# Second layer's deformable sampling: nine products summed by transposes that accumulate in PSUM, tap weights by blocks of 128, x tents in PSUM

## The reference, cut to what matters

```python
xi = xg[:, :, :, g, :]
offsets = conv_same(xi, w_off[g], b_off[g])
# sample_with_offsets: loc = grid + kernel_grid + offsets, clipped to the image
interp = w_(wa) * Ia + w_(wb) * Ib + w_(wc) * Ic + w_(wd) * Id     # bilinear, 9 points x 16 channels
h = depthwise_same(sampled, w_dw[g], b_dw[g])                      # H x W x 144
outs.append(conv_same(h, w_pw[g], b_pw[g]))                        # 144 -> 16
```

## Time and profile before

| what | us |
|---|---|
| median of 3 runs (lowest, highest) | 295.47 (294.94, 296.95) |
| span of the profiled execution | 295.1 |
| PE busy over the span | 234.4 (79%) |
| DVE busy | 196.2 (66%) |
| POOL busy | 140.1 (47%) |
| ACT busy | 57.0 (19%) |

### The profile page before, as it was taken

One profiled execution on the slowest core, in us unless ns is written; L12 is line 12 of the kernel. 1 busy time (PEld: TensorE's weight loads), 2 busy tenths in 40 slices (PEclk: granted clock), 3 DMA queues, 4 the chain that ended last, 5 costly groups with the idle time before them and its releaser, 6 DMA issues.

```text
span 295.1 us, 2939 instructions
## 1 busy us (share of the span) xinstructions
PE 234.4 (79%) x908; PEld 134.6 (46%) x910; DVE 196.2 (66%) x476; ACT 57.0 (19%) x94; POOL 140.1 (47%) x196
## 2 busy tenths in 40 slices
PE   0959298988988789978883586889899788899990
PEld 0725096763336642224531142457578746343430
DVE  7767779979875387573309859998977144326286
ACT  1411924210001164513111000010101301310100
POOL 5300009786951509713404929999996010000560
PEclk9997969999996579999995769999999997799997
DMA  3529970000000000000166000000000000000000
GB/s 114 160 50 187 203 196 0 0 0 3 1 1 0 0 1 3 0 0 0 26 154 125 0 1 0 0 1 3 0 0 0 2 0 0 1 2 0 0 18 18
DMA packets 5759, 9.37 MB, mean 32 GB/s; under 512 B 2390, under 2 KB 2926, under 8 KB 5742
## 3 DMA queue, kind: packets, MB, share of 16 engines
q1 hardware_dynamic: 5742, 9.18, 13.3%
HBM read 7.48 MB, written 1.69 MB: 31 GB/s over the span
## 4 chain that ended last, share of the span: by engine, by line
PE 40%; DVE 30%; POOL 15%; issue 6%; ACT 5%; DMA 1%; DVEq 1%; POOLq 0%; ACTq 0%
POOL ring L265 12%; PE ps L1011 5%; PE ps L906 5%; PE ps L746 4%; PE ps L764 3%; DVE ps L1176 3%; PE ps L876 3%; DVE big L279 3%; PE ps L932 2%; DVE cm L1123 2%; DVE xn L1079 2%; PE ps L699 2%; PE ps L813 2%; DVE ring L287 2%; PE ps L727 2%
## 5 line engine op out<-in xcount | busy, mean ns | idle before, releaser
L265 POOL TENSOR_TENSOR ring<-big 128x384 f32<-128x384 f32 x72 | 59.2, 861 | 9.4 <-PE ps L906 4.6
L297 POOL TENSOR_TENSOR big<-big 128x512 f32<-128x512 f32 x30 | 32.0, 1095 | 38.6 <-ACT big L621 32.9
L906 PE MATMUL ps<-ring,ident 128*128 128x384 f32 x100 | 38.0, 523 | 10.2 <-POOL ring L265 5.7
L746 PE MATMUL ps<-ring,ident 128*128 128x192 f32 x126 | 26.4, 362 | 8.6 <-DVE ring L287 8.4
L1484 DVE TENSOR_TENSOR ps<-ps,ring 128x384 f32<-128x384 f32 x46 | 25.8, 562 | 9.6 <-PE ps L906 8.4
L906 PEld LDWEIGHTS ps<-ring,ident 128*128 128x128 f32 x100 | 19.1, 202 | 26.3 <-DVE ring L265 7.2
L746 PEld LDWEIGHTS ps<-ring,ident 128*128 128x128 f32 x126 | 22.6, 208 | 12.8 <-DVE ring L287 12.8
L433 POOL TENSOR_TENSOR rstd<-veps,mhalf 128x4 f32<-128x4 f32 x8 | 8.3, 1032 | 39.3 <-DVE veps L1075 39.2
L691 PE MATMUL ps<-zero,ident 128*128 128x512 f32 x34 | 22.7, 815 | 1.6 <-DVE big L1402 1.6
L554 POOL TENSOR_TENSOR big<-big 128x256 f32<-128x256 f32 (+1 forms) x12 | 7.6, 635 | 34.4 <-DVE big L1562 33.7
L265 DVE TENSOR_TENSOR ring<-big,ps 128x384 f32<-128x384 f32 x36 | 19.5, 546 | 0.1
(11 more groups left out here) (270 smaller groups left out, 397.5 us busy)
## 6 DMA issues: line engine op xcount, KB each, us to landing
big<-pad SPq DMA_DIRECT2D x8, 392.0 KB, 9.5
big<-pad SPq DMA_DIRECT2D x8, 240.0 KB, 5.5
w<-in_w_dram SPq DMA_DIRECT2D x2, 512.0 KB
w<-in_w_dram SPq DMA_DIRECT2D x2, 256.0 KB
pad<-img SPq DMA_DIRECT2D x8, 64.0 KB, 2.1
pad<-zero SPq DMA_DIRECT2D x1, 484.0 KB, 3.9
pad<-zero SPq DMA_DIRECT2D x1, 400.0 KB, 4.5
x<-in_x_dram SPq DMA_DIRECT2D x1, 256.0 KB, 2.6
```

The costliest lines, as they stand in the source:

```text
L265: return eng.tensor_tensor(V(ring, 0, slot * SP, [[1, P], [NJ * C, 3], [C1, NJ * G1], [1, C1]]), bigv((py + dy) * SLAB1 + (dx + j0) * C, [ ...
L297: return eng.tensor_tensor(dst, bigv(wy * SLAB0 + wx * C, [C0, J * G0], [1, C0]), table, ALU.mult)
L746: return mm(bank(px + dx, 0, P, [1, 3 * J * G0], off=dy * J * G0), ident[:, :], ring[:, slot + 3 * px * J * G0:slot + 3 * (px + 1) * J * G ...
L906: mm(bank(1 + i % 2, 0, P, [1, SP]), ident[:, :], ring[:, slot * SP:slot * SP + SP], start=(n == 0), stop=(n == len(srcs) - 1)).then_inc(s ...
```

## The change

The items are gone. A chunk of two columns is handled whole: nine terms, one for each shift d, each with all nine points of both columns. A term is two products of 576 numbers per partition (`sample_product`, one for each column), written so that the group's 9 x 16 samples lie in one run of 144. Five shifts are on DVE (0 to 4), four on POOL (5 to 8): 40 and 32 products. Nothing is added on DVE. PE instead transposes every term and lets the transposes accumulate in PSUM: per term nine 128 x 128 blocks (`add_term`, L896 of the changed file), in the order of `TERMS`; banks 1, 2 and 3 hold the chunk's nine transposed blocks, ACT copies them after the ninth term, and the next chunk's first term waits for these copies.

The blocks of 128 rows cut across the runs of 144, so that each group and column lies in two adjoining blocks. `taps_out` (L925 of the changed file) has two products for each, 16 per chunk, with weights `w_u` laid out by blocks, zero outside. Twelve of a chunk's 16 are put between the terms of the next chunk by `TAPS_BY`, four come after it.

The tents: the x tents are written to PSUM (bank 4), so that `pair_weights` reads one operand from SBUF and one from PSUM. The lower tent is left negative and the sign is put in by a `scalar_tensor_tensor` with -1. A partition with an offset over 1 gets weight 0 (`near`), which adds two one-number operations and one of 576. The reduction of the largest offset stands ahead of the pairs instead of behind them; POOL's product with -1 goes away. The two weight loads (52 KB, and twice 6.5 KB) become one of 209 KB (128 x 408 numbers), at the same place in SP's order; POOL's preparation becomes one product of 2304 numbers and two of 64.

```diff
+            def transposed_sum(dst, columns, first, last):
+                return mm(dst, columns, ident[:, :], is_transpose=True, start=first, stop=last, skip_group_check=True)
+            def add_term(ci, t):
+                who = TERMS[t]
+                k = ci * TERMS.count(who) + TERMS[:t].count(who)
+                first, last = t == 0, t == len(TERMS) - 1
                 for n in range(NJ):
+                    if first and ci:
+                        pe.wait_ge(sem("st"), (NJ + 1) * (ci - 1) + n + 1)
+                    pe.wait_ge(sem("s_pool" if who == "pool" else "s_dve"), NJ * k + n + 1)
                     for g in range(G1):
+                        done = transposed_sum(bank(1 + n, 0, P, [1, P], off=g * P),
+                                              term_slot(who, k, (n * G1 + g) * P, [1, P]), first and g == 0, last)
+                    if last:
+                        done.then_inc(sem("st_ps"), 1)
+                if first and ci:
+                    pe.wait_ge(sem("st"), (NJ + 1) * ci)
+                done = transposed_sum(bank(3, 0, P, [1, P]), term_slot(who, k, NJ * G1 * P, [1, P]), first, last)
+                done.then_inc(sem("s_pe"), 1)
...
             pe.wait_ge(sem("tents1"), 1)
             keep_clock(3, 3)
+            for ci in range(NC):
+                if ci > 1:
+                    for part in range(TAPS_BY[-1], TAP_PARTS):
+                        taps_out(ci - 2, part)
+                for t in range(len(TERMS)):
+                    add_term(ci, t)
+                    if ci:
+                        for part in range(TAPS_BY[t], TAPS_BY[t + 1]):
+                            taps_out(ci - 1, part)
+            for part in range(TAPS_BY[-1], TAP_PARTS):
+                taps_out(NC - 2, part)
+            for part in range(TAP_PARTS):
+                last = taps_out(NC - 1, part)
+            last.then_inc(sem("u_ps"), 1)
...
-            v.scalar_tensor_tensor(bigv(T1 + 2 * NT, [1, NT]), u1[:, :], 0.0, val1[:, :], ALU.max, ALU.mult)
-            dve.wait_ge(sem("neg_val1"), 1)
-            v.scalar_tensor_tensor(bigv(T1, [1, NT]), u1[:, :], 0.0, ml[:, :], ALU.min, ALU.mult)
+            for dst, half in ((x_tent1, of_x), (y_tent, of_y)):
+                v.scalar_tensor_tensor(dst(2), u1[:, half], 0.0, fx[:, half], ALU.max, ALU.mult)
+                v.scalar_tensor_tensor(dst(0), u1[:, half], 0.0, fx[:, half], ALU.min, ALU.mult)
...
-SP = 3 * NJ * C
+SP = NJ * K * C
-S_DVE = (0, 1, 2)
-S_POOL = (3, 4, 5, 6, 7, 8)
+POOL_SLOTS, DVE_SLOTS = 4, 5
+S_DVE = (0, 1, 2, 3, 4)
+S_POOL = (5, 6, 7, 8)
+TERMS = ("pool", "dve", "pool", "dve", "dve", "pool", "dve", "dve", "pool")
+TAP_PARTS = 2 * NJ * G1
+TAPS_BY = (0, 0, 2, 4, 5, 6, 8, 9, 10, 12)
```

More of the change, by code:

```diff
@@ L125, in program @@
         flagf = sb("flagf", P, 4)
+        near = sb("near", P, 2)
         flagi = sb("flagi", 1, 4, dt=I32)
@@ L202, in program @@
         aby = sb("aby", P, J * GP0)
-        BIG = 19760
+        BIG = 18432
         big = sb("big", P, BIG)
@@ L275, in pair_weights, with y_tent, x_tent1 @@
+        def y_tent(k):
+            return bigv(T1 + k * J * GP1, [1, J * GP1])
+        def x_tent1(k):
+            return bank(4, 0, P, [1, J * GP1], off=k * J * GP1)
         def pair_weights(eng, d):
             dy, dx = divmod(d, 3)
[L278 to L281, removed]
+            dst = bigv(AD + d * J * GP1, [1, J * GP1])
+            if (dy == 0) != (dx == 0):
+                pair = eng.scalar_tensor_tensor(dst, y_tent(dy), -1.0, x_tent1(dx), ALU.mult, ALU.mult)
+            else:
+                pair = eng.tensor_tensor(dst, y_tent(dy), x_tent1(dx), ALU.mult)
+            pair.then_inc(sem("pairs"), 1)
@@ L335, in _ @@
             load(b_of[:, :], "b_of", "w_of")
-            load(w_ta[:, :], "w_ta", "w_dp")
-            for hf in range(2):
-                load(w_tb[C * hf:C * hf + C, :], "w_tb", "w_dp")
+            load(w_t[:, :], "w_t", "w_dp")
             load(b_tb[C:C + 1, :], "b_pw", "w_dp")
@@ new lines, in add_term, with taps_out @@
+                done.then_inc(sem("s_pe"), 1)
+            def taps_out(ci, part):
+                ng, tail = part % (NJ * G1), part // (NJ * G1)
+                n, g = divmod(ng, G1)
+                j = NJ * ci + n
+                block = ng + tail
+                if part in (0, G1, TAP_PARTS - 1):
+                    pe.wait_ge(sem("st"), (NJ + 1) * ci + (1, 2, 3)[block // G1])
+                return mm(bank(4 + g, 0, P, [1, K * C1], off=j * 3 * C1), bigv(ST + (ci * 9 + block) * P, [1, P]),
+                          w_u[:, (ng * 2 + tail) * K * C1:(ng * 2 + tail + 1) * K * C1], start=(j == 0 and tail == 0),
+                          stop=(j == J - 1 and tail == 1), skip_group_check=True)
@@ L1511, in _ @@
+                sampling(general=True)
+            with dve.Else():
+                sampling(general=False)
             dve.wait_ge(sem("u_ps"), 1)
@@ L1776 @@
     b_dw = i["L1_conv_b_dw"].reshape(G1, K, C1).transpose(1, 2, 0)
-    w_ta = np.concatenate([t[:8].reshape(P, -1) for t in (w_dw, w_pw, b_dw)], axis=1)
-    w_tb = np.concatenate([np.moveaxis(t[8], 1, 0).reshape(C, -1) for t in (w_dw, w_pw, b_dw)], axis=1)
+    w_t = np.zeros((3, P, 2 * NJ * G1, C1), np.float32)
+    for ng in range(NJ * G1):
+        for e in range(K * C1):
+            block, row = divmod(ng * K * C1 + e, P)
+            part, (p, c) = 2 * ng + block - ng, divmod(e, C1)
+            w_t[0, row, part, :K] = w_dw[p, c, ng % G1]
+            w_t[1, row, part] = w_pw[p, c, ng % G1]
+            w_t[2, row, part, 0] = b_dw[p, c, ng % G1]
+    w_t = np.concatenate([w_t[0, :, :, :K].reshape(P, -1), w_t[1].reshape(P, -1), w_t[2, :, :2 * G1, 0]], axis=1)
     data = {
```

323 lines of the change are left out of this document (91 added, 232 removed).

## The result

The changed kernel takes **280.52 us** (median of 5 executions, 278.67 to 281.08) against 294.94 us before (5 executions, 293.1 to 296.95) on the same chip: ratio 0.951, 95% interval 0.9456 to 0.9564. The prediction was 279.5 us, with 275 to 290 as its range.

The account below looks back on a forecast made before the run. The prediction took POOL's 72 products to bound the old stage and PE the new one. Moving the last tap from 234.3 to 218.3 us saves 16.0: 295.1 - 16.0 = 279.1 us span, 279.5 against the median, range 275 to 290.

Parts of the forecast that it names:

- The bound and its size: Sampling: PE becomes the bound at 12.8 us per chunk; last tap at 218.3 against 234.3 us, 16.0 us less.
- The far end: Upper bound for one POOL product of 576 numbers in the sampling: 1.6 us, for addressing in four dimensions.
- POOL idle waiting for PE, over 3 us per chunk: Sign expected in the sampling's trace: POOL stands idle behind PE for over 3 us in each chunk.
- Pairs: DVE's nine pair products before the sampling: 0.39 us each, 3.5 us instead of 7.9.
- if that cure fails they cost 7.9 again: Fallback for DVE's nine pairs: without the gain from a PSUM operand they take 7.9 us, 4.4 more.
- The branch: Flag and branch between pairs and copy of weights: 0.65 us, bounds 0 and 1.3, against 1.45 before.
- keep_clock: PE's start of the sampling, when keep_clock is done: 5.3 us after the tents, at 166.3 us.
- What was to cost nothing: Larger weight load, under 1 us if uncovered; POOL's preparation of 4.6 us, ready early; work after the last tap unchanged.
- Clock falls under transposes: Rival, sampling: PE's clock drops to 0.50 and stays there, last tap at 263, total 328 us; chance 0.13.
- It falls in the first chunk: Rival: PE's clock drops only in the first chunk, without taps between transposes; 7.3 us more, 287 us; chance 0.07.
- Weight loads as the pace: Rival, PE's transposes: each goes at its weight load's 0.14 us; 9.7 us more, 289 us; chance 0.05.
- POOL the bound: Rival, sampling: POOL's products take above 1.6 us and still bound it; at 1.8 us the total is 285; chance 0.02.

Follow-up runs that it names:

- e8: Changed kernel with only the split of the nine products moved, VectorE four and POOL five instead of five and four: 279.57 us, ratio 0.9499.
- e3: Changed kernel with the three x tents in SBUF instead of PSUM, all else the same: 281.49 us, ratio 0.9526.
- e1: Changed kernel without the three 512-column products on zeros (keep_clock) ahead of the sampling: 281.07 us, ratio 0.9501.
- e2: Changed kernel with all 64 taps behind the last transpose, so 324 transposes in a row: 280.12 us, ratio 0.9496.
- e6: Changed kernel with VectorE adding two of its five products of a chunk in SBUF, so PE sums eight terms: 279.65 us, ratio 0.9505.
- e7: Changed kernel with VectorE taking six products, POOL three, each adding one pair in SBUF; PE sums seven terms: 280.73 us, ratio 0.9554.
- e4: Kernel before with only the x tents moved to PSUM, in six tent operations instead of three: 288.81 us, ratio 0.9782.
- e5: Changed kernel with POOL adding two of its four products of a chunk in SBUF, so PE sums eight terms: 276.00 us, ratio 0.9402.

## Why the prediction was right

- **The bound and its size.** PE was to be the bound at 12.8 us a chunk, with a last tap 16.0 us earlier. The profile has a chunk's distance of 184.57 to 197.35 = 12.8 us, and 16.75 us. Transposes were priced at 0.11 and measure 0.109 (9 in 0.98); 44 tap records in 5.41 us are 0.246 a tap, priced at 0.245.
- **POOL.** Priced at 1.16 a product from one row of the same size, and measured 1.17. The far end, 1.6, is nowhere near; addressing in four dimensions costs nothing here. e8 shows that five products still fit. One sign of the list failed, without harm to the time: "POOL idle waiting for PE, over 3 us per chunk" measured 3.3 us in the whole stage. The slots were taken as full from the start. POOL needs some 9.1 us a chunk (31.79 us for 28 products) against PE's 12.8, so it gains 3.7 us a chunk, and four slots, a whole chunk's worth of its terms, let it run ahead nearly to the end; that reading is worked out from these rows, no run varies the slots.
- **DVE.** 0.69 a product, measured 6.73 / 10 = 0.67. It was to wait for PE, and does.
- **Pairs.** 0.39 each, measured 0.37. The reason given (operands in SBUF against POOL) is right as a mechanism, but its fallback was mis-sized: "if that cure fails they cost 7.9 again". e3 takes the cure away and the stage loses 1.1 us, on POOL and not on DVE. In the kernel before the same part is worth 6.4 us.
- **The branch.** I took 0.65 us between nothing and 1.3. The pairs end at 162.81 and the copy of weights starts at 162.92, so it is 0.1: the flag was there 3 us earlier. With DVE's products at 0.67 this brings DVE's first term forward, which the first chunk needs.
- **`keep_clock`.** 5.3 us taken from the old kernel; here the first transpose starts 4.7 us behind it. These two terms are most of the 0.75 us by which the stage came out shorter.
- **The total.** 279.5 predicted, 280.5 measured, though the stage gained more than predicted. The weak step is the last one: the span of one execution of the kernel before, 295.1, was set 0.4 us from the median, when its own time was some 1.8 us above its span, the highest of all. The forecast gain of 16.0 us came out as 14.4 by medians. So the total is as close as it is in part by luck: a stage that gained 0.75 us more than forecast, and a whole time that gained 1.6 us less. Both differences are smaller than the 2 to 4 us by which executions of one kernel differ.
- **What was to cost nothing.** The larger weight load stayed covered: POOL's first product on the first layer's slab still waits 31.0 us for ACT, and the part behind the last tap is as long as before. The stretch at half clock there, which the forecast let vanish for up to 3 us, stayed at 6.9 us in both profiles of the changed kernel.
- **Rivals.** Clock falls under transposes: refuted by e1 and e2, over 36 us. It falls in the first chunk: doesn't happen in the changed kernel, but e6 and e7 show how near it is, since a wait of 2 us there brings it. Weight loads as the pace: refuted. POOL the bound: refuted by e8.

What stays open: which of the two engines loses when both read SBUF, how the 10.3 us beyond e4 divide among their parts, and why the half-speed stretch behind the last tap lasts 3.4 us in one kernel's profile and 7 in the others'.

## What to carry to other kernels

Sum products where an engine can add in passing: letting the transposes accumulate took 25.8 us of additions from DVE, and the room that this made there took a third of POOL's products away from it, for 0.98 us of PE a term. Then count all three engines again, because the new bound can be shared out too, but only by an operation whose price on that engine has been measured; beside a busy POOL, VectorE's product with one operand in PSUM (0.67 us) and its sum of two in SBUF (1.27) are not the same thing. And value a part of a change in the kernel in which it is to stand: the same placement was worth 6.4 us in one and 1.1 in the other.

## What the runs showed of the hardware that I had not expected

- Transposes in float32 alone raise the granted clock from 0.50 to 1.00 (e1, at about 168.4 us) and hold it (e2). A transpose of 128 x 128 costs 0.109 us at the high clock, and nine take about 2 us at the low one.
- While DVE ran nine products back to back with both operands in SBUF, a product on POOL lasted 3.81 us instead of 1.17, and DVE lost nothing (e3).
- Sums of two SBUF operands of 576 numbers: on DVE 0.75 us when POOL was done, and up to 1.72 beside a busy POOL (e6, e7); 1.42 on POOL, whose product of the same size takes 1.17.
- Two waits of PE, of 1.05 and 0.98 us, were followed by some 3.4 us at half clock (e6); waits of 0.55 and 0.71 were not (e5).
